# A two-layer hybrid block with routed experts: token additions cut in four, expert weights asked for at the up products, rows turned three tiles ahead

## The reference, cut to what matters

```
x = h                                    # 8 x 512 tokens of 128 numbers, float32
x = x + attention_a(layernorm(x))        # causal, 16 heads
x = x + experts(layernorm(x))            # expert stage 0
x = x + attention_b(layernorm(x))        # over the 16 heads of one token
x = x + experts(layernorm(x))            # expert stage 1

def experts(x):                          # 24 experts, 512 hidden numbers, two per token
    scores = x @ gate_w + gate_b
    top2, gates = top_k(scores, 2), softmax(top2 values)
    y_e = gelu(x @ w1[e] + b1[e]) @ w2[e] + b2[e]
    return x + sum of gate * y_e over the two chosen experts
```

## Time and profile before

| | us |
|---|---|
| time, median of 3 runs | 1144.99 (1138.14 to 1148.18) |
| the profiled execution's own time | 1149.68 |
| its span, first to last instruction | 1147.9 |
| outside the span | 1.8 |
| TensorE clock granted, mean | 0.941 of full |

### The profile page before, as it was taken

How to read it: one execution, slowest core, us unless ns; L and a number is a source line. 1 busy time by engine, 2 the same in 40 slices (tenths; PEclk the granted TensorE clock), 3 DMA queues, 4 the chain that set the end, 5 groups by cost and what they waited for, 6 DMA issues and landing times.

```text
span 1147.9 us, 28676 instructions
## 1 busy us (share of the span) xinstructions
PE 984.6 (86%) x9446; PEld 768.5 (67%) x9446; DVE 776.9 (68%) x2149; ACT 698.0 (61%) x2115; POOL 734.1 (64%) x1065
## 2 busy tenths in 40 slices
PE   4999999999999934999999899888898817999995
PEld 2555555555555524998998577766776717999994
DVE  3688878888788652445454688899999763444543
ACT  3578787877877731655555567677666424555552
POOL 8646476767666334656666767688898563655564
PEclk8699999999999976999999799999999958999998
DMA  9999980000000004677775999990000015778774
GB/s 344 407 405 405 357 287 30 14 16 14 13 10 21 20 17 125 200 196 221 213 205 157 353 406 408 407 303 17 21 12 19 21 43 174 206 218 236 219 218 120
DMA packets 121849, 203.13 MB, mean 177 GB/s; under 512 B 13281, under 2 KB 67225, under 8 KB 121575
## 3 DMA queue, kind: packets, MB, share of 16 engines
q1 hardware_dynamic: 111446, 184.08, 48.1%
q0 software_dynamic: 9728, 16.95, 4.4%
q10 hardware_dynamic: 528, 0.26, 0.1%
HBM read 76.72 MB, written 127.65 MB: 178 GB/s over the span
## 4 chain that ended last, share of the span: by engine, by line
PE 34%; POOL 21%; issue 19%; DVE 19%; ACT 4%; DMA 1%; POOLq 1%; DVEq 0%; SPq 0%; ACTq 0%
POOL rows_out L890 15%; PE bank L1494 6%; PE bank L1107 6%; PE bank L1455 5%; PE bank L1415 3%; POOL SETTLE L889 3%; DVE QK L1209 3%; DVE NMP L1674 3%; PE bank L1436 2%; PE bank L1410 2%; PE bank L1473 2%; POOL rows_in L700 1%; DVE NMP L1670 1%; DVE PT L1220 1%; PE bank L583 1%
## 5 line engine op out<-in xcount | busy, mean ns | idle before, releaser
L918 ACT ACTIVATE QT<-bank,B 128x128 f32<-128x128 f32 x704 | 201.7, 368 | 195.5 <-PE bank L940 195.5
L890 POOL DMA_INDIRECT rows_out<-Y,XI x176 | 179.3, 1019 | 87.2 <-POOL SETTLE L889 80.9
L1616 ACT ACTIVATE PT<-bank 128x512 f32<-128x512 f32 x320 | 188.1, 603 | 68.3 <-PE bank L1436 67.9
L940 PE MATMUL bank<-XIT,PT 128*128 128x128 f32 x1408 | 193.0, 281 | 4.6 <-DVE XIT L992 3.8
L951 PE MATMUL bank<-W,QT 128*128 x1408 | 187.2, 276 | 1.3 <-ACT QT L918 1.3
L1044 POOL TENSOR_TENSOR PT<-PT 128x512 f32<-128x512 f32 x128 | 158.5, 1269 | 40.7 <-ACT PT L1150 40.7
L940 PEld LDWEIGHTS bank<-XIT,PT 128*128 128x128 f32 x1408 | 174.2, 195 | 9.4 <-DVE XIT L992 6.5
L951 PEld LDWEIGHTS bank<-W,QT 128*128 128x128 f32 x1408 | 171.5, 192 | 1.6 <-issue 1.6
L700 POOL DMA_INDIRECT rows_in<-XG,POS x128 | 126.6, 989 | 47.5 <-issue 33.2
L1455 PE MATMUL bank<-KT,QT 48*128 48x384 bf16 (+3 forms) x512 | 122.2, 310 | 10.5 <-DVE NMP L1670 8.6
L997 DVE TENSOR_TENSOR YB<-bank,B2R 128x128 f32<-128x128 f32 x176 | 51.3, 291 | 113.6 <-PE bank L951 113.3
(11 more groups left out here) (220 smaller groups left out, 2024.3 us busy)
## 6 DMA issues: line engine op xcount, KB each, us to landing
rows_in<-XI SPq DMA_DIRECT2D x32, 3120.0 KB, 30.8
PT<-in_w_dram SPq DMA_DIRECT2D x176, 256.0 KB
XI<-rows_in SPq DMA_DIRECT2D x176, 65.0 KB
PT<-rows_out SPq DMA_DIRECT2D x31, 256.0 KB, 4.5
W<-in_w2pack_dram SPq DMA_DIRECT2D x4, 1536.0 KB, 15.2
rows_in<-XI SPq DMA_DIRECT2D x2, 1560.0 KB, 31.1
rows_out<-Y,XI POOLq DMA_INDIRECT x176, 3.4
X<-in_h_dram SPq DMA_DIRECT2D x8, 256.0 KB, 4.8
```

Source lines behind the costliest of these rows:

```text
L890: pool.indirect_dma_start(out=rows_out, out_offset=bass.IndirectOffsetOnAxis(ap=XI_I[:, u, D + 1:D + 2], axis=0), in_=Y[:, u % 4, :], in_o ...
L918: a = act.activation(HT[:, u % 2, c, :], psH[u % 2][:, c * P:(c + 1) * P], ACT.Gelu, bias=B1[:, bass.ds(e * FC + c, 1)])
L940: mm = pe.matmul(psH[u % 2][:, c * P:(c + 1) * P], W1[:, u, c * P:(c + 1) * P], XIT[:, u % 2, :], start=True, stop=True)
L1616: act.activation(PT[:, m % PT_SLOTS, :], psB[m % 2][:, :], ACT.Exp, scale=float(D) ** -0.5).then_inc(exp_done, 1)
```

## The change

Four edits, all in the expert stages.

1. Turning: PE turns rows three tiles ahead (`turn(j + 3)`), DVE copies three tiles ahead; psXI and XIT get a third buffer (bank 6 of PSUM, 64 KB of SBUF). Before the first up product three tiles are turned instead of two. down(j) gets a wait of its own for the bias of tile j - 2 (f_biased), since the old order no longer assures it.
2. Loads: weights of tile j + 3 are asked for in SP's body of tile j, before the wait on the results of tile j - 8, once up(j - 5), the last reader of that weight buffer, is done (f_up). Rows j are asked for where they were. At the start of a stage the order is: weights 0 to 3, the waits for routing, rows 0, weights 4, rows 1, weights 5, and so on; the batch of rows 0 to 3 is gone.
3. Additions: the two additions of a group become four over 128x256, one after each of tiles 8g + 36 to 8g + 39. The statistics of groups 0 and 1 are cut over three tiles from four tiles after combine_at, their last step one tile later; POOL's power follows at + 10 instead of + 6. f_done counts halves.
4. Output: a group is sent two tiles later (8g + 47), and the last group in two halves of 128 KB.

```diff
@@ -48,7 +48,8 @@
 STEP = 8
 READ_AT = 4
-STEP_FIRST = 4
+WEIGHTS_AHEAD = 3
+TURN_AHEAD = 3
 SPIN_TURNED, SPIN_QUERIES, SPIN_EXPS = 2, 2, 18
 ROW_TILES = STEP * -(-((2 * TOKENS - NE) // P + NE) // STEP)
 GROUPS = TILES // GT
@@ -71,7 +72,7 @@
 def send_at(g):
-    return fetch_at(g) + 7
+    return fetch_at(g) + 9
 W2_EXPERTS = 6
 NOWHERE = 2 * 2 * TOKENS
@@ -181,7 +182,7 @@
         YB = sb("YB", [P, 2, D])
         XI = sb("XI", [P, STEP, ROW_W])
         XI_I, XG_I = (x.bitcast(I32) for x in (XI[:, :, :], XG[:, :, :, :, :]))
-        XIT = sb("XIT", [D, 2, P])
+        XIT = sb("XIT", [D, 3, P])
         weights = PT[:, :, :].rearrange("p s t -> p (s t)")
         in_keys = weights[:, 0:STEP * FF]
@@ -322,7 +323,8 @@
         LG, CAND = choice(0, GT, NE), choice(9 * NE, GT, NE)
         O1H = [FIRST, choice(13 * NE, GT, NE)]
         TOP2, IDX, POSF = choice(17 * NE, GT), choice(GT * NE, GT), choice(GT * NE, GT, 2)
-        psXI, psH, psY = banks[0:2], banks[2:4], banks[4:6]
+        psXI = [banks[i][:, 0:P] for i in (0, 1, 6)]
+        psH, psY = banks[2:4], banks[4:6]
         psP, psF, psS = banks[0:2], banks[2], banks[4:6]
         EX = [banks[i][:, 0:H * H].rearrange("p (h g) -> p h g", h=H) for i in (3, 6)]
@@ -817,7 +819,7 @@
         def fetch(eng, ph, g, k):
             if 4 <= g < GROUPS - 1:
-                eng.wait_ge(f_done, ph * GROUPS + g - 3)
+                eng.wait_ge(f_done, 2 * (ph * GROUPS + g - 3))
             eng.dma_start(arrived(g)[:, k, :, :],
                           rows_out_v[:, k, g * GT:(g + 1) * GT, :]).then_inc(f_yc[g], 16)
@@ -837,22 +839,23 @@
             def load(j, u):
+                if j == 0:
+                    for i in range(WEIGHTS_AHEAD):
+                        load_weights(i, i)
+                if WEIGHTS_AHEAD <= j + WEIGHTS_AHEAD < ROW_TILES:
+                    if j + WEIGHTS_AHEAD >= STEP:
+                        sp.wait_ge(f_up, base + j + WEIGHTS_AHEAD - STEP + 1)
+                    load_weights(j + WEIGHTS_AHEAD, (u + WEIGHTS_AHEAD) % STEP)
                 sent_before(sp, ph, j, STEP)
-                if j == STEP_FIRST:
-                    for i in range(STEP_FIRST):
-                        load_weights(i, i)
+                if j == 0:
                     emptied(sp, ph, GROUPS // 2 - 1)
                     for par in range(2):
                         sp.wait_ge(r_scat[par], 16 * GT * GROUPS * (ph + 1))
-                    for i in range(STEP_FIRST):
-                        load_rows(i, i)
-                if j >= STEP_FIRST:
-                    load_rows(j, u)
-                    load_weights(j, u)
-            def send_group(g):
-                sp.wait_ge(f_done, GROUPS + g + 1)
-                sp.dma_start(out_v[:, g * GT:(g + 1) * GT, :], X[:, g * GT:(g + 1) * GT, :]).then_inc(out_sent, 16)
+                load_rows(j, u)
+            def send_tiles(T0, T1):
+                sp.wait_ge(f_done, 2 * GROUPS + T1 // 2)
+                sp.dma_start(out_v[:, T0:T1, :], X[:, T0:T1, :]).then_inc(out_sent, 16)
             def body(j, u):
                 load(j, u)
@@ -861,7 +864,7 @@
                         fetch(sp, ph, g, 0)
                         fetch(sp, ph, g, 1)
                     if ph == 1 and j == send_at(g):
-                        send_group(g)
+                        send_tiles(g * GT, (g + 1) * GT)
             over_rows(body, read_ahead(sp, f"sp_number{ph}", (EJ, NE - 1), (RJ, DUMMY)))
@@ -874,9 +877,11 @@
                 for c in range(GROUPS // 2):
                     empty_rows(sp, 1, c)
             if ph == 1:
-                for g in range(GROUPS):
+                for g in range(GROUPS - 1):
                     if send_at(g) >= ROW_TILES:
-                        send_group(g)
+                        send_tiles(g * GT, (g + 1) * GT)
+                send_tiles(TILES - GT, TILES - 2)
+                send_tiles(TILES - 2, TILES)
         def experts_pool(pool, ph):
@@ -891,7 +896,7 @@
                                         in_=Y[:, u % 4, :], in_offset=None, bounds_check=2 * TOKENS - 1,
                                         oob_is_err=False).then_inc(f_ys[u], 16)
                 for g in range(2):
-                    if ph == 0 and j == combine_at(g) + 6:
+                    if ph == 0 and j == combine_at(g) + 10:
                         group_power(pool, GROUPS + g, g)
             over_rows(body)
@@ -931,21 +936,21 @@
             def turn(j, u):
                 pe.wait_ge(f_load[u], per_buffer(ph, j, 2))
-                pe.transpose(psXI[u % 2][:, 0:P], XI[:, u, 0:D], IDF[:, :]).then_inc(f_xiT, 1)
+                pe.transpose(psXI[j % 3], XI[:, u, 0:D], IDF[:, :]).then_inc(f_xiT, 1)
             def up(j, u):
                 pe.wait_ge(f_xit, base + j + 1)
                 for c in range(FC):
-                    mm = pe.matmul(psH[u % 2][:, c * P:(c + 1) * P], W1[:, u, c * P:(c + 1) * P], XIT[:, u % 2, :],
+                    mm = pe.matmul(psH[u % 2][:, c * P:(c + 1) * P], W1[:, u, c * P:(c + 1) * P], XIT[:, j % 3, :],
                                    start=True, stop=True)
                 mm.then_inc(f_up, 1)
             def down(j, u):
                 e = tile_number(j)
-                if j + 1 >= ROW_TILES:
-                    pe.wait_ge(f_y, base + j - 1)
+                if base + j >= 2:
+                    pe.wait_ge(f_biased, base + j - 1)
                 pe.wait_ge(f_gelu, base + j + 1)
                 for c in range(FC):
                     mm = pe.matmul(psY[u % 2][:, 0:D], HT[:, u % 2, c, :],
@@ -956,8 +961,8 @@
             def body(j, u):
                 if j + 1 < ROW_TILES:
                     up(j + 1, (u + 1) % STEP)
-                if j + 2 < ROW_TILES:
-                    turn(j + 2, (u + 2) % STEP)
+                if j + TURN_AHEAD < ROW_TILES:
+                    turn(j + TURN_AHEAD, (u + TURN_AHEAD) % STEP)
                 down(j, u)
             pe.wait_ge(e_flat, ph + 1)
@@ -967,21 +972,28 @@
             mm.then_inc(e_turned, 1)
             pe.wait_ge(e_tables, ph + 1)
             pe.wait_ge(w2_in, 16 * (NE // W2_EXPERTS + 1))
-            turn(0, 0)
-            turn(1, 1)
+            for i in range(TURN_AHEAD):
+                turn(i, i)
             up(0, 0)
             over_rows(body, read_ahead(pe, f"pe_expert{ph}", (EJ, NE - 1)))
-        def combine(eng, ph, g):
-            n = ph * GROUPS + g
-            x = tiles_at(X, GT * g, GT)
-            y = arrived(g)
-            wait(eng, f_done, n)
-            eng.wait_ge(f_yc[g], 32 * (ph + 1))
-            eng.tensor_tensor(y[:, 0], y[:, 0], y[:, 1], ALU.add).then_inc(f_ysum, 1)
-            eng.wait_ge(f_ysum, n + 1)
-            eng.tensor_tensor(x, x, y[:, 0], ALU.add).then_inc(f_done, 1)
+        def add_fetched(dve, ph, g, half):
+            y = arrived(g)[:, :, 2 * half:2 * half + 2]
+            if half == 0:
+                dve.wait_ge(f_yc[g], 32 * (ph + 1))
+            dve.tensor_tensor(y[:, 0], y[:, 0], y[:, 1], ALU.add).then_inc(f_ysum, 1)
+        def add_to_tokens(dve, ph, g, half):
+            dve.wait_ge(f_ysum, 2 * (ph * GROUPS + g) + half + 1)
+            x = tiles_at(X, GT * g + 2 * half, 2)
+            dve.tensor_tensor(x, x, arrived(g)[:, 0, 2 * half:2 * half + 2], ALU.add).then_inc(f_done, 1)
+        def combine(dve, ph, g, step):
+            (add_fetched, add_to_tokens)[step % 2](dve, ph, g, step // 2)
         def experts_dve(dve, ph):
             base = ph * ROW_TILES
@@ -989,7 +1001,7 @@
             def xi_copy(j, u):
                 dve.wait_ge(f_xiT, base + j + 1)
-                dve.tensor_copy(XIT[:, u % 2, :], psXI[u % 2][:, 0:P]).then_inc(f_xit, 1)
+                dve.tensor_copy(XIT[:, j % 3, :], psXI[j % 3]).then_inc(f_xit, 1)
             def gated(j, u):
                 e = tile_number(j)
@@ -1000,26 +1012,30 @@
                 dve.tensor_scalar(Y[:, u % 4, :], YB[:, u % 2, :], XI[:, u, D:D + 1], None, ALU.mult).then_inc(f_y, 1)
             def body(j, u):
-                if j + 2 < ROW_TILES:
-                    xi_copy(j + 2, (u + 2) % STEP)
+                if j + TURN_AHEAD < ROW_TILES:
+                    xi_copy(j + TURN_AHEAD, (u + TURN_AHEAD) % STEP)
                 gated(j, u)
                 for g in range(GROUPS - 1):
-                    if j == combine_at(g):
-                        if g == 0:
-                            dve.wait_ge(r_xadd, GROUPS * (ph + 1))
-                        combine(dve, ph, g)
-                    if ph == 0 and g < 2 and j == combine_at(g) + 2:
-                        dve.wait_ge(f_done, g + 1)
-                        for i in range(6):
+                    step = j - combine_at(g)
+                    if g == 0 and step == 0:
+                        dve.wait_ge(r_xadd, GROUPS * (ph + 1))
+                    if 0 <= step < 4:
+                        combine(dve, ph, g, step)
+                    if ph == 0 and g < 2:
+                        if step == 4:
```

(18 more changed lines are left out.)

## The result

| | before | after |
|---|---|---|
| median of 4 runs each, us | 1145.42 | 1166.63 |
| lowest to highest | 1138.14 to 1148.18 | 1159.76 to 1170.20 |
| ratio, 95% interval | | 1.019 [1.012, 1.026] |
| profiled execution, its span | 1149.68, 1147.9 | 1170.20, 1168.5 |

A forecast was written before the change was run, and what follows sets the result against it. TensorE sets the pace, with 25.3 us lost in the expert stages. That loss becomes 15 (-10) and the starts add 4: -6 against 1149.68 gives 1143.7, as a median 1139 us; range 1127 to 1151.

The forecast's parts named there:

- L: Expert stages: the rows' own landing, from asking to turning; taken as 2.2 us, 1.87 seen at a stage's start.
- A + L > 6.58: Eight-tile circle of a row buffer: TensorE waits once this sum exceeds 6.58 us; before, 8.48 with the weights included.
- A: Start of a tile's scatter to the next rows asked for: medians 3.9 and 4.2 us, taken over unchanged.
- (c): Rows land late behind a fetch, L 4.5 us: 33 us lost instead of 25.3, 1157 with the start; chance 0.16.
- 14 clusters: Tiles of both stages with A above 5.0, peaks averaging 5.5 us; there turns would wait 15 us in all.
- the start: Start of each expert stage: first up product later, 2.0 us a stage, 4 for both, bounds 2.8 and 7.6.
- TensorE starts cold either way: Start of each expert stage: TensorE is cold before and after the change; no time was priced for it.
- The pieces' 6 us: Up products: additions in pieces and copies a tile earlier remove all waits on XIT, 6.0 us.
- The wait on f_up: SP's queue, in front of rows j: nearly always met, costing nothing unless results land a microsecond sooner than usual.
- Output sent later: Output two tiles later moves 256 KB from before a fetch to after the next rows: taken as 0, -2 to +2 us.
- Ring order: DMA ring: rows stand behind 256 KB of weights nobody needs yet; L 3.1, waits 28 us, time 1152.
- Too few buffers as the cause of a repeating gap: TensorE's gaps: by this rule the third buffer would fill them; the trace agreed only for 6 us of copy waits.

The follow-up runs named there:

- e3: Changed kernel with rows 0 to 3 asked for together ahead of weights 4 to 7: 1159.2 us, 1.011 to before.
- e4: Kernel before with the changed kernel's additions, statistics and output, plus an unused third bank and buffer; old loads, two tiles ahead: 1142.7 us, 1.000 to before.
- e1: Changed kernel with rows turned two tiles ahead again instead of three: 1135.6 us, 0.991 to before.
- e2: Changed kernel with the loads of before (weights behind rows, first four tiles together), still three tiles ahead: 1177.8 us, 1.026 to before.
- e10: Changed kernel, three tiles ahead, with nine row buffers instead of eight, rows 0 and 1 asked for together: 1133.5 us, 0.989 to before.
- e5: Changed kernel with the fetches of finished rows issued from ScalarE's queue instead of SP's: 1160.8 us, 1.014 to before.
- e7: Changed kernel with the two fetches of groups 0 to 6 cut from four tiles to one: 1153.2 us, 1.006 to before.
- e8: Changed kernel, three tiles ahead, with twelve row buffers instead of eight, rows 0 to 3 asked for together at the start: 1129.8 us, 0.988 to before.

## Why the prediction was wrong

**The step that failed: L.** "I take 2.2, near the quiet row, because weights j + 3 go out a tile's time ahead of rows j and have mostly passed: 14 x 1.1 = 15 us." The mechanism and its bound (wait once A + L > 6.58) were right; the term was sized with the quiet landing. Behind nine of 12 fetches L is 4.0 to 4.7, which is what rival (c) had worked out from one row of before (4.5), and dismissed as the worst of all. The text named the point from which (c) decides, 3.6, and then judged by the one row at the start of a stage, where the DMA engines are a quarter busy (0.25). With L at 4.5, (c)'s loss of 33 us is close to the 35.9 measured in the same way, though split otherwise: turn by turn 23.8 are lost behind the fetches, where it had 28, and 10.4 elsewhere, where it had 5, since L is mostly 3.4 to 4.3 in the late turns there too. The sum also looked for the waits where A peaks ("14 clusters" above 5.0); most came behind the fetches, where A is near its usual size (4.2) and L is not.

**The second term: the start.** Taken as 2.0 a stage, bounds 1.4 to 3.8; the two starts cost 4.4 and 4.3. The first up product came 3.8 and 2.1 later than before. The rest lies behind it and was not in the sum: the engine's granted clock rises later. Windows of 1 us of stage 1 (the clock is the third number from the end), of before:

```profile
956.00:957.00 1.00, 1.00 (x7) 1.00 (x6) 0.00 (x0) 0.81 (x4) 0.00 (x0) 0.50 0.75 172
957.00:958.00 1.00, 1.00 (x9) 1.00 (x9) 0.23 (x1) 0.57 (x3) 0.00 (x0) 0.82 0.98 321
```

and of after:

```profile
972.00:973.00 1.00, 1.00 (x7) 1.00 (x7) 0.22 (x1) 0.00 (x0) 0.00 (x0) 0.57 0.98 267
973.00:974.00 1.00, 1.00 (x12) 1.00 (x11) 0.51 (x3) 0.17 (x1) 0.19 (x1) 1.00 0.17 50
```

A mean of 0.82 between 0.50 and 1.00 puts the rise from 1.2 to 2.4 GHz at 957.4, 3.4 us behind the first up product (953.97), and one of 0.57 at 972.9, 6.0 us behind it (966.82). In stage 0 it is 4.6 and 5.7 us. So 2.7 us more at half clock in stage 1 and 1.0 in stage 0, or 1.3 and 0.5 us of work; 0.9 us in stage 1 stay unexplained. "TensorE starts cold either way" was true and beside the point: how long it stays cold changed. e3 shows the order of the transfers to be the cause: with rows first the start is 37.9 instead of 44.9 (36.2 before).

**Why (c)'s own 1157 fell short.** Its mechanism was priced +12: 7.7 for the waits (33 - 25.3) and 4 for the start. Measured by the same windows, the loss is 35.9 instead of 25.3, +10.6, and the start is +8.7. What is over is mostly the start.

**What was right.** The waits on XIT go to zero, a piece takes 0.42 us, the pace between waits stays 1.895. From a turn to the end of its y are 7.8 to 8.0 us in undisturbed tiles (7.8 worked out) and from there to the scatter 0.78. A has a median of 3.8 and 3.9 (3.9 and 4.2 before), so taking it over was sound. The pieces' 6 us were counted in full, though, and alone they give some 3 by the steady loss and none that the medians tell (e4). The gain of the early weights was put together with the third tile ahead and never priced by itself: it is 7 to 10 us with two ahead (e1 against e4), and 11 of steady loss with three (e2), less 8 for the start.

**What was wrong without consequence that can be seen.** The wait on f_up was to be "nearly always met". SP stood in it 20 times, 15.5 us in all. In the version with twelve buffers SP's list of waits doesn't show it, and it is shorter where turns are less late (5.9 us in e1, 4.5 in e10), which speaks for its following from late turns. A did not grow either. But no run takes it away alone, so its cost stays open. Output sent later was not tried by itself either; e4 holds it, at a ratio of 1.000.

**The rules cited.** Ring order, taken from the Trainium skill, page "DMA: Bandwidth & Descriptors", section "Queues, rings and completion order", was priced with only the weights in front: L of 3.1 and 1152. The landing was longer than that, and with the fetch in another ring (e5) it is no shorter, so the ring doesn't explain it. Too few buffers as the cause of a repeating gap (the Trainium skill, page "Perfetto Trace Analysis", section "Identifying Performance Opportunities") was taken as a rule in favour of the third bank and XIT buffer. It holds here for another ring, XI: one more row buffer takes 24 us away.

**The chances.** (c) had 0.16 and most of it was left out of the range, on the argument that its row was the worst of all, with an output transfer in front. The trace of before already spoke against that. An output transfer stands in front of every fetch of stage 1 but the first, and of the 12 turns behind a fetch seven ended a wait for the load, 4.5 to 6.2 us after the rows were asked for. By (c)'s own subtraction (1.7 us for the weights) that is an L of 2.8 to 4.5, and above 3.6 for five of the seven. Two of them, 6.15 and 5.72 us (rows asked for, turn):

```profile
1091.52 0.36 SPq L836 DMA_DIRECT2D XI<-rows_in  x1
...
1097.67 0.14 PEld L934 LDWEIGHTS bank<-IDF,XI 128*128 128x128 f32 x1 [0.69 <-DMA PT<-in_w_dram]
...
1108.07 0.35 SPq L836 DMA_DIRECT2D XI<-rows_in  x1
...
1113.79 0.14 PEld L934 LDWEIGHTS bank<-IDF,XI 128*128 128x128 f32 x1 [0.71 <-DMA PT<-in_w_dram]
```

The bad row was the rule for its kind of tile, and these are just the tiles where the waits lie after the change.

## What to carry to other kernels

Looking one tile further ahead at a stage that shares a ring of buffers with the output shortens the time in which the ring can be refilled by one tile; count the whole circle (hold, drain, wait, landing) and give the ring a buffer for each tile of lookahead. Size a transfer's landing in such a sum by the busiest place at which it must be in time, not by the quiet one, and if the decision hangs on it, look at the other tiles of the bad row's kind before calling it the worst. Read the DMA share over the few microseconds of that transfer, since a window over the whole stage averages it away. At the start of a stage, ask first for what the first products need; the bulk that is needed four tiles later goes behind.

## What the runs showed of the hardware

A 65 KB transfer that lands in 1.9 us where the DMA share is 0.25 takes 4.0 to 4.7 us, nine times of 12, with 512 KB of other transfers asked for just before it, and 3.8 to 5.5 if these stand in another engine's queue (e5, nine of 12). The share between asking and turning is then 0.88 to 1.02 (changed kernel, eleven of 12). The slow landing also comes without a whole fetch: in e7, behind the one that took 2.79, the next rows took 4.27:

```profile
527.54 0.36 SPq L839 DMA_DIRECT2D XI<-rows_in  x1
...
531.81 0.14 PEld L940 LDWEIGHTS bank<-IDF,XI 128*128 128x128 f32 x1 [0.46 <-DMA XI<-rows_in]
```

The share over these two is 0.69 and 0.84. It isn't the whole of it: away from the fetches of the changed kernel, eight landings of 3.4 to 4.3 us come with shares of 0.57 to 0.78.

The granted clock of TensorE rose from the lower to the upper of its two levels (1.2 and 2.4 GHz) 3.4 to 6.0 us behind the first up product of a stage in before and after, and 2.3 us behind it in stage 0 of e8 (447.34 to 449.66), although in the stage where it took longest (stage 1 of after) the engine was busy without a gap from 967 us on. Between the two expert stages it fell and rose several times, and it was at the lower level for 50 us in the shortest such stretch (e7, 322.4 us) and for 78.5 in the longest (e2, 335.1).
